# Second attention of a small transformer on one core: the scores of four heads from one 512-column product with keys widened by zeros

## The chip, the cores and the metric

One core of a Trainium2 chip runs the whole program. The metric is the device time of that core in microseconds (us); the median of several executions is used.

## The reference, cut to what matters

Input x is 8 batches of 128 tokens by 128 features, and a context of the same shape goes with it. Four blocks follow each other, each added to x: a channel attention, a mixture of 16 experts with a causal attention, the second attention (this case), and a feed-forward block with 8 routed experts. The change touches only the second attention:

```python
def _L1_xattn_ref(k, q, v, Wk, bk, Wq, bq, Wc, bc):   # k = v = context, q = layernorm(x)
    H, hd = 16, 8
    kp = k @ Wk.T + bk
    qp = q @ Wq.T + bq
    kh = kp.reshape(B, T_v, H, hd).transpose(0, 2, 1, 3)
    qh = qp.reshape(B, T_q, H, hd).transpose(0, 2, 1, 3)
    vh = v.reshape(B, T_v, H, hd).transpose(0, 2, 1, 3)
    att = jnp.einsum('bhqd,bhkd->bhqk', qh, kh) / sqrt(hd)
    att = jax.nn.softmax(att, axis=-1)
    y = jnp.einsum('bhqk,bhkd->bhqd', att, vh)
    return y.transpose(0, 2, 1, 3).reshape(B, T_q, C) @ Wc.T + bc
```

Here B is 8 and T is 128, so each batch has 16 heads of 8 features, with a 128 x 128 table of scores for each.

## The kernel before, in words

**Layout.** Each head of 8 features takes 32 rows (partitions) of the tiles ks and qs: high part, low part and marks, so that a float32 product comes out of fp32r operands. Four heads j = 0 to 3 fill the 128 partitions, and g = 0 to 3 counts the four groups, so that ks and qs are 128 partitions x 8 batches x 4 groups x 128 tokens. quarter(j) is the slice of 32 partitions of head j in its group.

**What one batch b goes through in the second attention.**

- turn_q (L1534) turns the queries, and take_qs (ACT, L690) writes them to qs.
- scores3(h), h = 2b + p with p = 0 or 1, is called once for each half of a batch (L1549). It computes the scores with queries on the partitions; they serve only to find the largest score of each row. A half is the two heads j = 2p and 2p + 1 of all four groups: eight products, each 32 rows of contraction and 128 columns. The two heads of a half go to two PSUM banks.
- softmax3(h) (DVE, L1144) reduces the two banks to the negated maxima negm. split_m (L1155, L1156) puts them as high and low part into msp.
- mark_queries (L1559, L1562) adds the maxima as extra rows to the queries, and take_marked (ACT, L705) writes qs again.
- turned_scores(h) (L1576) computes the scores again, now with keys on the partitions, in the same eight row-tiled products; exp3 (ACT, L700) takes the exponential into exT.
- attend3 (L1589, column tiles of 32), turn_y (L1596), divide (DVE), turn_divided (L1602), bring_x and project_c (L1611, L1615) end the batch.

**What sets the order.** Every engine's order is written out by hand: a counter s runs over all slots, and a function is called on its engine when s equals at_mix(b, u), at_score(b, u) or at_att(b, u). TensorE (PE) takes scores3(2b) at at_score(b, 0) and scores3(2b + 1) at at_score(b, 8). From batch 3 on, the first half's scores stand directly ahead of turned_scores of an earlier batch's second half, both behind attend3. The engine waits on semaphores in this order.

**Work of the expert block that shares time.** load_rwb (L416) and load_rwm (L424) on the SP queue bring router weights that are broadcast over the partitions from HBM: 1 MB and 0.5 MB for each batch. scale_hidden (DVE, L1099) multiplies by the first, mix(b) (DVE, L1131) by the second; project (L1476) and project_o (L1514) are the products on PE. load_rwm(7) waits for mix(6). The SP queue runs its steps strictly in turn, so a step that waits holds all steps behind it. GpSimd (POOL) is mostly busy with split_weights (L533). Its memsets (L512 to L517) stand ahead of its own loop.

Of the kernel before, what the change touches and what calls it, by code (L numbers as in the profile page):

```python
# [62 lines left out]
def build(nc, x_d, ctx_d, ctxT_d, cols_d, rows_d, kv_d, wattn_d, wqkv_d, wo_d, wa_d, wb_d, wdn_d, wg_d, out_d):  # L63
    starts, ends = {}, {}
    with ExitStack() as ctx:
# [12 lines left out]
        def sem(name):  # L78
            return ctx.enter_context(nc.semaphore(name))
# [100 lines left out]
        ry = sb("ry", [T, H1])  # L180
        yq = sb("yq", [T, H1, D1])
        yT = sb("yT", [C, 2, T])
        vT = exT[:, 0, :, :].rearrange("p a n -> p (a n)").rearrange("p (v n) -> p v n", v=2)
        bd = exT[:, 1, :, :].rearrange("p a n -> p (a n)").rearrange("p (f v i n) -> p f v i n", f=2, v=2, i=HALF)

# [63 lines left out]
        s2_ps = sem("s2_ps"); s2_ready = sem("s2_ready"); p2_ready = sem("p2_ready"); pn_ready = sem("pn_ready")  # L249
        pT2_ps = sem("pT2_ps"); pT2_ready = sem("pT2_ready"); aT_ps = sem("aT_ps"); aT_ready = sem("aT_ready")  # L250
        mix_ready = sem("mix_ready"); o_ready = sem("o_ready")
        kp_ready = sem("kp_ready"); ksT_ps = sem("ksT_ps"); ks_ready = sem("ks_ready")
        xn3_ready = sem("xn3_ready"); xn3T_ps = sem("xn3T_ps"); xn3T_ready = sem("xn3T_ready")
        qp_ready = sem("qp_ready"); qsp_ready = sem("qsp_ready"); qsT_ps = sem("qsT_ps"); qs_ready = sem("qs_ready")
# [44 lines left out]
        def routed_chunk(r):  # L299

            return (r - 1) // NROUTED * NCH + NSHARED + (r - 1) % NROUTED

        def rwm_of(b):

# [30 lines left out]
        def quarter(j):  # L335

            return slice(32 * j, 32 * j + 32)

        def score_bank(j):

            return 4 + 3 * (j % 2)
# [42 lines left out]
        @block.sync  # L384
        def _(sp):
            sp.dma_start(xr[:, bs(0), :], x_d[:, bs(0), :]).then_inc(ld_x[0], 16)
            sp.dma_start(cx[:, bs(0), :], ctx_d[:, bs(0), :]).then_inc(ld_ctx[0], 16)
            sp.dma_start(xr[:, bs(1), :], x_d[:, bs(1), :]).then_inc(ld_x[1], 16)
            sp.dma_start(cx[:, bs(1), :], ctx_d[:, bs(1), :]).then_inc(ld_ctx[1], 16)
            sp.dma_start(rowv[:, :], rows_d.partition_broadcast(128)).then_inc(ld_vec, 16)  # L390
            sp.dma_start(cxT[:, :], ctxT_d).then_inc(ld_ctxT, 16)
            sp.dma_start(wattn[:, :, :], wattn_d).then_inc(ld_attn, 16)
            sp.dma_start(wqkv[:, :, :], wqkv_d).then_inc(ld_qkv, 16)
            sp.dma_start(wo[:, :, :], wo_d).then_inc(ld_o, 16)
            sp.dma_start(wa[:, :], wa_d).then_inc(ld_up, 16)
            sp.dma_start(wb[:, :], wb_d).then_inc(ld_up, 16)
            sp.dma_start(wg[:, :], wg_d).then_inc(ld_up, 16)
            full = RUP // 128
            sp.dma_start(wdn[:, 0:full, :], wdn_d[0:full * 128, :].rearrange("(k p) c -> p k c", p=128)).then_inc(ld_dn, 16)
            sp.dma_start(wdn[0:RUP - full * 128, full, :], wdn_d[full * 128:RUP, :]).then_inc(ld_dn, 16)  # L400

            def store_rw(hf):

                rows_of = slice(HALF * E0 * hf, HALF * E0 * hf + HALF * E0)
                sp.wait_ge(rwT_ready, hf + 1)
                sp.dma_start(rw_d[rows_of, :], rwT[:, hf, :]).then_inc(rw_stored, 16)
                sp.wait_ge(rw_stored, 16 * (hf + 1))

            def load_rwb(b):

                if b < HALF:
                    sp.wait_ge(att_ready, 2)
                else:
                    sp.wait_ge(hm_ready, 4 * (b - 1))
                for q in range(4):
                    sp.dma_start(rwb[b % 2][:, 4 * q:4 * q + 4, :].rearrange("p e t -> p (e t)"),  # L416
                                 rw_d[E0 * b + 4 * q:E0 * b + 4 * q + 4, :].rearrange("e t -> (e t)").partition_broadcast(128)).then_inc(ld_rwb[b % 2][q], 16)

            def load_rwm(b):

                if b >= 2:
                    sp.wait_ge(mix_ready, b if b == NB - 1 else b - 1)
                for j in range(2):
                    sp.dma_start(rwm[rwm_of(b)][HD * j:HD * j + HD, :, :],  # L424
                                 rw_d[E0 * b:E0 * b + E0, :].rearrange("(r j) t -> j r t", j=2)[j, :, :].partition_broadcast(HD)).then_inc(ld_rwm[rwm_of(b)], 16)

            store_rw(0)
            load_rwb(2)
            load_rwb(3)
            load_rwm(0)  # L430
            load_rwm(1)
            store_rw(1)
            for b in range(HALF, NB):
                load_rwb(b)
                load_rwm(b - 2)
            load_rwm(NB - 2)
            load_rwm(NB - 1)

            def store_ww(hf):

                sp.wait_ge(wwT_ready, hf + 1)
                sp.dma_start(ww_d[E1 * hf:E1 * hf + E1, :].rearrange("e (b t) -> (e b) t", t=T), wwT[:, hf, :]).then_inc(ww_stored, 16)
                sp.wait_ge(ww_stored, 16 * (hf + 1))

            def load_ww(r):

                if r > BY_PE + 3:
                    sp.wait_ge(hid_ready, routed_chunk(r - 3) + 1)
                else:
                    sp.wait_ge(qkv_done, 4 * NB)  # L450
                for e, p, n in experts_of(r):
                    sp.dma_start(ww[p:p + n, r % 3, :], ww_d[E1 * ((r - 1) // NROUTED) + e, :].partition_broadcast(n)).then_inc(ld_ww[r % 3], 16)

            def store_out(hf):

                sp.wait_ge(out_ready, hf + 1)
                sp.dma_start(out_d[:, 512 * hf:512 * hf + 512], outT[:, hf, :]).then_inc(stored, 16)

            store_ww(0)
            for r in range(BY_PE + 1, NROUTED + 1):  # L460
                load_ww(r)
            store_ww(1)
            for r in range(NROUTED + 1, NROUTED + 4):
                load_ww(r)
            store_out(0)
            for r in range(NROUTED + 4, 2 * NROUTED + 1):
                load_ww(r)
            store_out(1)
            sp.wait_ge(stored, 32)
# [3 lines left out]
        def _(pool):  # L473
# [42 lines left out]
            link(nc.gpsimd.memset(vm[:, :, :, :], 0.0))  # L516
            link(nc.gpsimd.memset(vm[:, :, :, D1:D1 + 1], 1.0))  # L517

            def fill_vm(b):

                if b >= 2:
                    pool.wait_ge(pv_done, b - 1)
                nc.gpsimd.tensor_copy(vm[:, b % 2, :, 0:D1], cx[:, b, :].rearrange("p (h i) -> p h i", i=D1)).then_inc(vm_ready, 1)
# [29 lines left out]
                low_part(hlo[0:n, k % 3, :], hid[0:n, k % 3, :], hhi[0:n, k % 3, :]).then_inc(hlo_ready, 1)  # L553

            for s in range(LAST):
                for b in range(NB):
                    if s == at_mix(b, 82):
                        rstd_of(b + 1, 2, b, b + 1, ve_mix, rstd_mix)
                    if s == at_mix(b, 102):
                        add_bc(b)  # L560
                    if s == at_att(b, 4):
                        fill_vm(b)
                    if s == at_att(b, 44):
                        rstd_of(b + 1, 3, b, b + 1, ve_att, rstd_att)
                if s % SLOT == 0 and 0 <= s // SLOT - W4 < NCH:
                    split_weights(s // SLOT - W4)
                for hf in range(2):
                    if s == at_tail(hf, 72, 120):
                        split_x4(hf)
                for k in range(2):  # L570
                    if s == at_first(k, 8):
                        split_hidden(k)
                if s % SLOT == 0 and 2 <= s // SLOT - F4 - 1 < ON_POOL:
                    split_hidden(s // SLOT - F4 - 1)
# [275 lines left out]
        def _(dve):  # L850
# [288 lines left out]
            def softmax3(h):  # L1139
                b, p = h // 2, h % 2  # L1140
                dve.wait_ge(s3_ready, h + 1)
                if b >= 2:
                    dve.wait_ge(msp_ready, b - 1)
                V.tensor_reduce(negm[:, b % 2, 2 * p:2 * p + 2, :], score_pair.rearrange("p j (g k) -> p j g k", g=4),  # L1144
                                AX.X, ALU.max, negate=True).then_inc(mx3_ready, 1)

            def split_m(b):
# [3 lines left out]
                else:  # L1151
                    dve.wait_ge(qm_ps, b)
                dve.wait_ge(mx3_ready, 2 * b + 2)
                hi, lo = [msp[:, :, :, 3 * D1 + i].rearrange("p g j -> p j g") for i in range(2)]
                link(V.tensor_copy(hi, negm[:, b % 2, :, :]))  # L1155
                V.tensor_tensor(lo, negm[:, b % 2, :, :], hi.bitcast(F32), ALU.subtract).then_inc(msp_ready, 1)  # L1156

# [152 lines left out]
        def _(pe):  # L1310
# [226 lines left out]
            def scores3(h):  # L1537
# [6 lines left out]
                else:  # L1544
                    pe.wait_ge(mx3_ready, h)
                pe.wait_ge(qs_ready, b + 1)
                for g in range(4):
                    for j in (2 * p, 2 * p + 1):
                        last = mm(PB[score_bank(j)][:, T * g:T * g + T], qs[quarter(j), b, g, :], ks[quarter(j), b, g, :], start=True, stop=True)  # L1549
                last.then_inc(s3_ready, 1)  # L1550

            def mark_queries(b):
# [286 lines left out]
```

## Time and profile before

| | us |
|---|---|
| median of 3 runs | 237.09 (236.08 to 237.65) |
| the profiled execution | 236.62 |
| its span, first to last instruction | 234.8 |
| TensorE (PE) busy | 211.8 (90%) |
| VectorE (DVE) busy | 166.5 (71%) |
| ScalarE (ACT) busy | 112.5 (48%) |
| GpSimd (POOL) busy | 95.3 (41%) |

The mean granted TensorE clock is 0.96 of full speed. To read it: busy time says which engine has most to do, and the chain of work that ended last says what set the end. A piece of the chain is counted from the end of the piece ahead of it to its own end; so the length of a PE piece includes what the engine lost between the two. DMA issues are shown by the queue that issues them (SPq) with the time that the issue took, and elsewhere with the time from issue to landing.

### The profile page before, as it was taken

The page shows a single profiled execution, that of the slowest core. Times are in us where ns is not written, and L with a number is a line of the kernel's source. Part 1 is how long each engine was busy: PE and PEld are TensorE (multiplying, and loading weights), DVE is VectorE, ACT ScalarE, POOL GpSimd, SP SyncE. Part 2 cuts the span into 40 slices and gives each one's busy share as a digit, 9 for nine tenths or more (in the row PEclk, how much of TensorE's full clock was granted, in tenths as well). Part 3 has the DMA queues.
Part 4 walks back from the last instruction along what each step waited for, and adds up shares of the span by engine and source line. Part 5 has one row for each costly group of instructions (what it writes and reads, how often), then busy time and mean ns, then how long its engine had stood idle before and what let it go on. Part 6 is the DMA issues. An engine that isn't in the chain of part 4 may idle for free.

```text
span 234.8 us, 4985 instructions
## 1 busy us (share of the span) xinstructions
PE 211.8 (90%) x1767; PEld 180.2 (77%) x1767; DVE 166.5 (71%) x495; ACT 112.5 (48%) x259; POOL 95.3 (41%) x127
## 2 busy tenths in 40 slices
PE   1398669999999999999799999998699999999994
PEld 0356549999999998988579888887577887888872
DVE  3598797669977989858792687865765688265753
ACT  0435432423264462422263777678453745555552
POOL 7143100150096999810411021122336655655660
PEclk9999957999999999999976999999999999999998
DMA  6997000398199953300300000000024430163401
GB/s 188 349 419 228 3 6 0 96 289 155 60 260 245 242 190 89 81 12 0 89 4 0 3 3 0 3 4 0 3 48 89 122 101 6 42 189 133 152 27 45
DMA packets 19256, 23.33 MB, mean 99 GB/s; under 512 B 1792, under 2 KB 12192, under 8 KB 19104
## 3 DMA queue, kind: packets, MB, share of 16 engines
q1 hardware_dynamic: 18896, 22.94, 34.3%
q8 instruction: 14, 0.23, 0.4%
q10 hardware_dynamic: 336, 0.08, 0.2%
q14 instruction: 10, 0.08, 0.1%
HBM read 22.39 MB, written 0.62 MB: 98 GB/s over the span
## 4 chain that ended last, share of the span: by engine, by line
PE 83%; DVE 7%; ACT 3%; DMA 2%; issue 2%; ACTq 1%; POOL 0%; DVEq 0%
PE psum L1476 19%; PE psum L1657 17%; PE psum L1713 8%; PE psum L1514 7%; PE psum L1576 3%; PE psum L1589 3%; PE psum L1549 3%; DMA kv<-kv_dram 2%; PE psum L1386 2%; PE psum L1342 2%; PE psum L1491 1%; PE psum L1534 1%; PE psum L1562 1%; PE psum L1596 1%; PE psum L1504 1%
## 5 line engine op out<-in xcount | busy, mean ns | idle before, releaser
L488 POOL TENSOR_TENSOR rstd<-ve,m 128x1 f32<-128x1 f32 (+1 forms) x20 | 14.2, 712 | 96.9 <-DVE ve L872 96.8
L1476 PE MATMUL psum<-wqkv,hm 128*128 128x192 f32 x256 | 47.8, 335 | 0.0
L533 POOL TENSOR_TENSOR qs<-hm,qs 128x512 fp32r<-128x512 f32 (+1 forms) x26 | 33.9, 1302 | 22.3 <-ACT qs L746 22.1
L1476 PEld LDWEIGHTS psum<-wqkv,hm 128*128 128x128 f32 x256 | 42.3, 195 | 0.1
L1144 DVE TENSOR_REDUCE negm<-psum 128x8 f32<-128x1024 f32 x16 | 19.6, 1222 | 7.7 <-PE psum L1549 7.6
L1713 PE MATMUL psum<-qs,wdhi 128*128 128x512 f32 (+1 forms) x56 | 21.8, 401 | 0.1
L1212 DVE TENSOR_TENSOR hm<-hm,psum 128x512 f32<-128x512 f32 x19 | 13.0, 686 | 11.3 <-POOL qs L533 5.0
L700 ACT ACTIVATE exT<-psum 128x1024 f32<-128x1024 f32 x16 | 16.4, 1024 | 7.5 <-PE psum L1576 7.0
L1099 DVE TENSOR_TENSOR hm<-xn2T,exT 128x512 f32<-128x512 f32 x24 | 19.6, 817 | 0.1
L746 ACT ACTIVATE qs<-hm 128x512 fp32r<-128x512 f32 (+1 forms) x28 | 17.5, 627 | 3.3 <-DVE hm L1215 2.0
L765 ACT ACTIVATE psum<-psum 128x512 f32<-128x512 f32 x19 | 11.1, 583 | 16.5 <-PE psum L1657 16.3
L1514 PE MATMUL psum<-wo,mixT 128*128 128x128 f32 x128 | 17.4, 295 | 0.1
L1514 PEld LDWEIGHTS psum<-wo,mixT 128*128 128x128 f32 x128 | 16.6, 209 | 0.3 <-issue 0.2
L1215 DVE TENSOR_TENSOR hm<-hm,psum 128x512 f32<-128x512 f32 x19 | 13.1, 688 | 2.0
L1713 PEld LDWEIGHTS psum<-qs,wdhi 128*128 128x128 f32 (+1 forms) x56 | 10.5, 188 | 3.4 <-DVE qs L1231 0.9
L1131 DVE TENSOR_TENSOR mixT<-aT,rwm 128x1024 f32<-128x1024 f32 x8 | 10.5, 1317 | 2.8 <-issue 1.5
L1657 PE MATMUL psum<-x4hi,wahi 128*128 128x512 f32 (+1 forms) x28 | 12.0, 427 | 0.0
L1576 PE MATMUL psum<-qs,ks 32*128 32x128 f32 x128 | 10.8, 287 | 1.1 <-ACT qs L705 0.9
L1713 PE MATMUL psum<-qs,wdlo 128*128 128x512 f32 (+1 forms) x28 | 11.1, 397 | 0.0
L1657 PE MATMUL psum<-x4lo,wahi 128*128 128x512 f32 (+1 forms) x28 | 11.1, 396 | 0.0
L1657 PE MATMUL psum<-x4lo,wbhi 128*128 128x512 f32 (+1 forms) x28 | 11.1, 395 | 0.0
L1657 PE MATMUL psum<-x4hi,wblo 128*128 128x512 f32 (+1 forms) x28 | 11.0, 393 | 0.0
(235 smaller groups left out, 487.8 us busy)
## 6 DMA issues: line engine op xcount, KB each, us to landing
exT<-rw_rows SPq DMA_DIRECT2D x24, 256.0 KB, 4.8
rwm<-rw_rows SPq DMA_DIRECT2D x16, 256.0 KB, 5.8
hm<-ww_rows SPq DMA_DIRECT2D x7, 256.0 KB, 3.3
wqkv<-wqkv_dram SPq DMA_DIRECT2D x1, 1536.0 KB, 10.5
hm<-ww_rows SPq DMA_DIRECT2D x4, 224.0 KB, 3.3
wa<-wa_dram SPq DMA_DIRECT2D x1, 880.0 KB, 12.9
wb<-wb_dram SPq DMA_DIRECT2D x1, 880.0 KB, 13.3
wdn<-wdn_dram SPq DMA_DIRECT2D x1, 832.0 KB, 15.0
```

Source lines behind the costliest of these rows:

```text
L488: nc.gpsimd.tensor_tensor(dst, src, m16[:, 0:src.shape[1]], ALU.pow).then_inc(signal, 1)
L533: return nc.gpsimd.tensor_tensor(dst, src, hi.bitcast(F32), ALU.subtract)
L700: nc.scalar.activation(exT[:, b % 2, 2 * p:2 * p + 2, :], turned_pair, ACT.Exp).then_inc(ex_ready, 1)
L746: nc.scalar.activation(hhi[0:n, k % 3, :], hid[0:n, k % 3, :], ACT.Copy).then_inc(hhi_ready, 1)
L1099: V.tensor_tensor(hm[:, b % 2, 4 * q:4 * q + 4, :], bc(xn2T[:, b, :], 1, 4), weights, ALU.mult).then_inc(hm_ready, 1)
L1144: V.tensor_reduce(negm[:, b % 2, 2 * p:2 * p + 2, :], score_pair.rearrange("p j (g k) -> p j g k", g=4), AX.X, ALU.max, negate=True).then_ ...
L1215: V.tensor_tensor(hid[:, k % 3, :], hid[:, k % 3, :], PB[gate_bank(k)][:, :], ALU.mult).then_inc(hid_ready, 1)
L1476: last = mm(bank[:, 0:3 * HD], hm[:, b % 2, e, :], wqkv[:, e, :], start=(e == 0), stop=(e == E0 - 1))
L1514: last = mm(PB[5][:, 0:C], mixT[:, r, :], wo[:, r, :], start=(r == 0), stop=(r == E0 // 2 - 1))
L1576: last = mm(PB[turned_score_bank(j)][:, T * g:T * g + T], ks[quarter(j), b, g, :], qs[quarter(j), b, g, :], start=True, stop=True)
L1657: last = mm(bank[0:n, :], w[:, c0:c0 + n], x[:, cols4], start=(j == 0), stop=(j == 2))
L1713: last = mm(bank[:, :], w[0:n, ch, :], h[0:n, k % 3, :], start=(ch == 0 and j == 0), stop=(ch == NCH - 1 and j == 2))
```

## The change

scores3 no longer multiplies head by head. For each batch there is a widened copy of the keys, in which head j of group g stands on its own 32 partitions in columns 128j to 128j + 127, and everything else is zero. One product of all 128 rows of qs for group g with the 512 columns of the widened keys gives the four heads of that group. A half is now two groups (g = 2p, 2p + 1), that is two products of 128 x 128 x 512 in place of eight of 32 x 128 x 128. The PSUM banks are the same two, with group and head exchanged; softmax3 and split_m follow that order. turned_scores is unchanged.

The widened keys have two buffers, one for even and one for odd batches: kd0, new, and kd1, in two halves over cxT and sel, which are no longer used by then. GpSimd zeroes them once: kd0 with its other memsets, kd1 at slots 56 and 60. The SP queue copies the keys from ks into the diagonal blocks (widen_keys): four DMAs of 64 KB for an even batch, eight of 32 KB for an odd one. Batches 0 and 1 are copied between the load_rwb and load_rwm of batches 4 and 5, the others behind load_rwm(7); from batch 2 on a copy waits until the scores of the batch before last are done (s3_ready).

```diff
--- before.py
+++ after.py
@@ -180,6 +180,8 @@
         ry = sb("ry", [T, H1])
         yq = sb("yq", [T, H1, D1])
         yT = sb("yT", [C, 2, T])
+        kd0 = sb("kd0", [128, 4, 4, T], F32R)
+        kd1 = [over("kd1a", [128, 2, 4, T], F32R, "cxT"), over("kd1b", [128, 2, 4, T], F32R, "sel")]
         vT = exT[:, 0, :, :].rearrange("p a n -> p (a n)").rearrange("p (v n) -> p v n", v=2)
         bd = exT[:, 1, :, :].rearrange("p a n -> p (a n)").rearrange("p (f v i n) -> p f v i n", f=2, v=2, i=HALF)
 
@@ -249,6 +251,7 @@
         s2_ps = sem("s2_ps"); s2_ready = sem("s2_ready"); p2_ready = sem("p2_ready"); pn_ready = sem("pn_ready")
         pT2_ps = sem("pT2_ps"); pT2_ready = sem("pT2_ready"); aT_ps = sem("aT_ps"); aT_ready = sem("aT_ready")
         mix_ready = sem("mix_ready"); o_ready = sem("o_ready")
+        kd_zero = sem("kd_zero"); ld_kd = [sem(f"ld_kd{i}") for i in range(2)]
         kp_ready = sem("kp_ready"); ksT_ps = sem("ksT_ps"); ks_ready = sem("ks_ready")
         xn3_ready = sem("xn3_ready"); xn3T_ps = sem("xn3T_ps"); xn3T_ready = sem("xn3T_ready")
         qp_ready = sem("qp_ready"); qsp_ready = sem("qsp_ready"); qsT_ps = sem("qsT_ps"); qs_ready = sem("qs_ready")
@@ -300,6 +303,10 @@
 
             return (r - 1) // NROUTED * NCH + NSHARED + (r - 1) % NROUTED
 
+        def wide_keys(b, g):
+
+            return kd1[g // 2][:, g % 2, :, :] if b % 2 else kd0[:, g, :, :]
+
         def rwm_of(b):
 
             return 0 if b in (1, 3, 5) else 1
@@ -424,6 +431,21 @@
                     sp.dma_start(rwm[rwm_of(b)][HD * j:HD * j + HD, :, :],
                                  rw_d[E0 * b:E0 * b + E0, :].rearrange("(r j) t -> j r t", j=2)[j, :, :].partition_broadcast(HD)).then_inc(ld_rwm[rwm_of(b)], 16)
 
+            def widen_keys(b):
+
+                if b >= 2:
+                    sp.wait_ge(s3_ready, 2 * b - 2)
+                else:
+                    sp.wait_ge(kd_zero, 2 * b + 1)
+                    sp.wait_ge(ks_ready, b + 1)
+                for j in range(4):
+                    src = ks[quarter(j), b, :, :].bitcast(F32)
+                    if b % 2:
+                        for i in range(2):
+                            sp.dma_start(kd1[i][quarter(j), :, j, :].bitcast(F32), src[:, 2 * i:2 * i + 2, :]).then_inc(ld_kd[1], 16)
+                    else:
+                        sp.dma_start(kd0[quarter(j), :, j, :].bitcast(F32), src).then_inc(ld_kd[0], 16)
+
             store_rw(0)
             load_rwb(2)
             load_rwb(3)
@@ -433,8 +455,13 @@
             for b in range(HALF, NB):
                 load_rwb(b)
                 load_rwm(b - 2)
+                if b < HALF + 2:
+                    widen_keys(b - HALF)
             load_rwm(NB - 2)
             load_rwm(NB - 1)
+            sp.wait_ge(ks_ready, NB)
+            for b in range(2, NB):
+                widen_keys(b)
 
             def store_ww(hf):
 
@@ -516,6 +543,17 @@
             link(nc.gpsimd.memset(vm[:, :, :, :], 0.0))
             link(nc.gpsimd.memset(vm[:, :, :, D1:D1 + 1], 1.0))
 
+            nc.gpsimd.memset(kd0[:, :, :, :].bitcast(F32), 0.0).then_inc(kd_zero, 1)
+
+            def zero_keys(i):
+
+                if i == 0:
+                    pool.wait_ge(kp_ready, 2)
+                    pool.wait_ge(vT_ready, 2)
+                else:
+                    pool.wait_ge(rb_ready, 8)
+                nc.gpsimd.memset(kd1[i][:, :, :, :].bitcast(F32), 0.0).then_inc(kd_zero, 1)
+
             def fill_vm(b):
 
                 if b >= 2:
@@ -553,6 +591,10 @@
                 low_part(hlo[0:n, k % 3, :], hid[0:n, k % 3, :], hhi[0:n, k % 3, :]).then_inc(hlo_ready, 1)
 
             for s in range(LAST):
+                if s == at_once(56):
+                    zero_keys(0)
+                if s == at_once(60):
+                    zero_keys(1)
                 for b in range(NB):
                     if s == at_mix(b, 82):
                         rstd_of(b + 1, 2, b, b + 1, ve_mix, rstd_mix)
@@ -1141,7 +1183,7 @@
                 dve.wait_ge(s3_ready, h + 1)
                 if b >= 2:
                     dve.wait_ge(msp_ready, b - 1)
-                V.tensor_reduce(negm[:, b % 2, 2 * p:2 * p + 2, :], score_pair.rearrange("p j (g k) -> p j g k", g=4),
+                V.tensor_reduce(negm[:, b % 2, 2 * p:2 * p + 2, :], score_pair.rearrange("p g (j k) -> p g j k", j=4),
                                 AX.X, ALU.max, negate=True).then_inc(mx3_ready, 1)
 
             def split_m(b):
@@ -1151,7 +1193,7 @@
                 else:
                     dve.wait_ge(qm_ps, b)
                 dve.wait_ge(mx3_ready, 2 * b + 2)
-                hi, lo = [msp[:, :, :, 3 * D1 + i].rearrange("p g j -> p j g") for i in range(2)]
+                hi, lo = [msp[:, :, :, 3 * D1 + i] for i in range(2)]
                 link(V.tensor_copy(hi, negm[:, b % 2, :, :]))
                 V.tensor_tensor(lo, negm[:, b % 2, :, :], hi.bitcast(F32), ALU.subtract).then_inc(msp_ready, 1)
 
@@ -1544,9 +1586,9 @@
                 else:
                     pe.wait_ge(mx3_ready, h)
                 pe.wait_ge(qs_ready, b + 1)
-                for g in range(4):
-                    for j in (2 * p, 2 * p + 1):
-                        last = mm(PB[score_bank(j)][:, T * g:T * g + T], qs[quarter(j), b, g, :], ks[quarter(j), b, g, :], start=True, stop=True)
+                pe.wait_ge(ld_kd[b % 2], (128 if b % 2 else 64) * (b // 2 + 1))
+                for g in (2 * p, 2 * p + 1):
+                    last = mm(PB[score_bank(g)][:, :], qs[:, b, g, :], wide_keys(b, g).rearrange("p j t -> p (j t)"), start=True, stop=True)
                 last.then_inc(s3_ready, 1)
 
             def mark_queries(b):
```

## Rows read from the trace of the kernel before

**Rows 1.** The page: its first line, and the chain that ended last, by engine.

```profile
span 234.8 us, 4985 instructions
...
PE 83%; DVE 7%; ACT 3%; DMA 2%; issue 2%; ACTq 1%; POOL 0%; DVEq 0%
```

**Rows 2.** Groups by shape, PE: busy us, mean ns of one | idle before.

```profile
L1549 PE MATMUL psum<-ks,qs 32*128 32x128 f32 x128 | 10.6, 283 | 0.0
```

**Rows 3.** Chain, 88 to 166 us: start, length, what; scores between other full-array products.

```profile
90.56 0.59 PE psum L1549 x8
91.16 0.26 PE psum L1500
...
103.47 0.11 PE psum L1500
...
151.89 0.23 PE psum L1559
...
152.52 0.59 PE psum L1549 x8
153.11 0.27 PE psum L1602
153.38 0.59 PE psum L1576 x8
```

**Rows 4.** The same chain: scores and turned scores together, and L1529 in two places.

```profile
99.42 0.22 PE psum L1529 x2
...
128.78 0.36 PE psum L1549 x4
...
129.36 0.18 PE psum L1576 x4
...
139.04 0.43 PE psum L1529 x2
...
150.05 0.37 PE psum L1549 x4
...
150.64 0.18 PE psum L1576 x4
```

**Rows 5.** Timeline of the SP queue, 65 to 69 us: start, length, what.

```profile
65.42 2.05 SPq L416 DMA_DIRECT2D exT<-rw_rows  x4
68.38 1.26 SPq L424 DMA_DIRECT2D rwm<-rw_rows  x2
```

**Rows 6.** Timeline of DVE, the first use of batch 5's router weights.

```profile
74.28 0.96 DVE L1099 TENSOR_TENSOR hm<-xn2T,exT 128x512 f32<-128x512 f32 x1
```

**Rows 7.** Timeline: the last load of router weights, and batch 2's first scores.

```profile
113.06 1.25 SPq L424 DMA_DIRECT2D rwm<-rw_rows  x2
...
117.37 0.66 PE L1549 MATMUL psum<-ks,qs 32*128 32x128 f32 x8
```

**Rows 8.** DMA, 111 to 120 us in 40 slices; its issues: KB each, us to landing.

```profile
GB/s 0 0 0 0 0 0 0 0 0 0 0 0 0 0 0 107 262 330 339 278 216 250 223 182 93 46 5 0 0 0 0 0 0 73 0 0 0 0 0 0
...
rwm<-rw_rows SPq DMA_DIRECT2D x2, 256.0 KB, 3.8
```

**Rows 9.** Source line L452, DMAs of 32 to 256 KB: issue ns min/median/max, then landing.

```profile
L452 SPq DMA_DIRECT2D hm<-ww_rows x31: 302/413/597, 173.5 to 221.5; - x31
...
DMA to landing us min/median/max: 1.9/3.1/4.8
```

**Rows 10.** Timeline of PE: second half of batch 3's scores, first half of batch 5's.

```profile
131.13 0.66 PE L1549 MATMUL psum<-ks,qs 32*128 32x128 f32 x8
...
139.39 0.33 PE L1549 MATMUL psum<-ks,qs 32*128 32x128 f32 x2
```

**Rows 11.** Timeline of POOL: a memset of 1024 columns, and its next work but one.

```profile
50.19 0.95 POOL L516 MEMSET vm<- 128x1024 f32 x1
...
64.16 0.85 POOL L488 TENSOR_TENSOR rstd<-ve,m 128x1 f32<-128x1 f32 x1 [12.80 <-DVE ve L872]
```

**Rows 12.** Windows, 123 to 127 us: busy by engine, granted clock, DMA share, GB/s.

```profile
123.00:127.00 4.00, 4.00 (x20) 3.77 (x21) 0.73 (x4) 0.60 (x1) 0.00 (x0) 0.50 0.00 0
```

## The prediction

> **What bounds the kernel now.** I read the page first: of a span of 234.8 us, PE makes up 83% of the chain that ended last [rows 1]. So a microsecond taken from PE's own sequence is a microsecond of the kernel, unless another engine stands in at that place. Then the groups by shape: the 128 score products of L1549 are 10.6 us of PE busy time [rows 2], but these overlap, so their price has to be read from the chain. The chain between 88 and 166 us shows L1549 in two settings. Nine times it is a piece of its own, 0.59 us for eight products, between or next to other work; the first and the last stand in [rows 3]. Four times it lies mixed with the eight products of turned_scores, because a half of scores and a half of turned scores stand next to each other in PE's order; the first and the last stand in [rows 4]. In the three that are left of 16 (two alone, one mixed) another engine sets the time. Last I read the SP queue and the DMA slices, since the change puts 48 new DMAs there [rows 5, 7, 8, 9].
>
> **The new products.** The trace has no 128-row product with widened keys, but it has the same form: L1559 takes fp32r queries as weights and 512 columns of fp32r, and its piece of the chain is 0.23 us [rows 3]. Two of them are 0.46 to 0.47 us in place of 0.59. That is 0.12 us less for a half. DVE's reduction has the same size and only another order, so I cost it at nothing; its input is complete about as early as before.
>
> **What a change of tiling costs.** Behind row tiles the next full-array product pays. L1500 behind the scores takes 0.26 us, and 0.11 behind a full product; L1602 takes 0.27 us behind the scores [rows 3], for a product of the same 128 columns. That is 0.15 us. The same holds behind the column tiles of L1589: L1529 takes 0.43 us there and 0.22 elsewhere [rows 4], 0.2 us more.
>
> **Where the scores stand alone on the path.** These are batches 0 and 1 (four halves), and the second halves of batches 4, 6 and 7. Each gives 0.12 us for itself and 0.15 for the product behind it, 0.27 us. Seven of them give 1.9 us. The other two of the nine lie at batch 2: its first half is followed by row-tiled L1576 after a wait, its second half directly by L1576, so the switch stays and I take nothing for them. The second halves of batches 3 and 5 are hidden behind ACT and DVE.
>
> **Where the scores stand with the turned scores.** Now 16 products need from 128.78 to 129.54 us, and again from 150.05 to 150.82: 0.77 us for both halves [rows 4]. In all such places the scores use heads 0 and 1 and the turned scores heads 2 and 3, so four row groups are in use together. The new scores fill the array, and nothing can share it: 0.47 us for the scores, then 0.59 us for turned scores alone, as at 153.38 [rows 3], is 1.06 us. In addition scores3 stands behind attend3 here, so a full-array product comes behind column tiles, for up to 0.2 us [rows 4]. Loss: 0.29 to 0.49 us; I take 0.45, since both places where the trace shows such a switch pay nearly the whole. Four on the path lose 1.8 us. The fifth (batch 5) lies behind DVE work and is hidden; were it not, another 0.45 us. The bound below is nothing: the matmul queue might still overlap the two.
>
> The Trainium skill, page TensorE: Matmul & The Clock Gate, Part 3, says that products with 32 rows of contraction run side by side in different row groups, four of them 3.07 times as fast as in turn, and so speaks against this change. By that rule eight products in two row groups, 128 columns each, would be worth about half of their row's time, some 0.3 us, and the change would lose 0.17 us at every half: with the switch the seven halves that stand alone would come to +0.1 us in place of -1.9. The rows don't bear that out for the halves that stand alone, since 0.59 us for eight is more than the 0.47 of two full products [rows 3]; they bear it out in part for the mixed places.
>
> **The first late copy of keys.** widen_keys(2) stands on SP behind load_rwm(7), which waits for mix(6) and ends its issues at 113.06 + 1.25 = 114.31 us [rows 7]. Four DMAs of 0.41 us (the median issue of L452 [rows 9]) occupy SP until 115.95, the last one starting at 115.54. Their data stand behind the 0.52 MB of load_rwm(7), which flow until slice 27 of 0.225 us, that is 117.0 us, in some 2.5 us, about 210 GB/s [rows 8]. 256 KB at this rate take 1.25 us: 118.3 us, and 0.3 to 0.5 us more until the semaphore. Batch 2's scores start at 117.37 us [rows 7] and would now start at about 118.7: **a stall of 1.3 us**. Behind it on PE are the turned scores of batch 0, the turn of batch 7's queries and project_o(7), all of which others wait for, and PE has no idle time behind it that would absorb it. Bounds: with the fastest landing of L452, 1.9 us [rows 9], the last lands at 117.4, no stall; with the slowest, 4.8 us, at 120.3, 3.0 us of stall. Gains upstream move mix(6), the load and the scores alike.
>
> **The later copies.** An odd batch takes eight issues. Batch 5's wait for the second half of batch 3's scores, done at 131.13 + 0.66 = 131.8 us; the last of eight issues starts at 134.7 and lands by 136.6 to 139.5, needed at 139.39 [rows 9, 10]. Batch 7 has the same distance, even batches half of the issues. So I cost them at nothing; even the slowest landing costs 0.1 us each. What hides them is 8.3 us of PE work between the two scores.
>
> **The early copies.** widen_keys(0) goes between load_rwm(2) and load_rwb(5), which was issued at 65.42 us [rows 5]: four issues, 1.6 us, and 256 KB, 1.2 us of traffic. widen_keys(1), 8 x 0.41 = 3.3 us, goes behind load_rwm(3) (68.38 [rows 5]). Batch 5's weights are used from 74.28 us on [rows 6], 8.9 us after their issue and now 7.3; the slowest landing there could make DVE some 0.5 us late, but PE's use is one scaling of 0.96 us and one project later, so nothing reaches the path. Bound above: 0.5 us.
>
> **Zeroing.** 1024 columns are 0.95 us, so kd0 and the two halves of kd1 are 1.9 + 2 x 0.95 = 3.8 us of POOL. POOL is idle for 12.8 us ahead of 64.16 [rows 11]. Nothing; without this cover, up to 3.8 us.
>
> **The sum.** -1.9 (alone) + 1.8 (mixed) + 1.3 (stall) = +1.2 us. The profiled execution took 236.62 us, 1.8 more than its span, and the median of the runs shown is 0.5 above it. So 236.6 + 1.2 = 237.8, and against the median 238.3; I say 238.0.
>
> **The rivals.**
>
> *Slower: the copy for batch 2 lands late.* For it: SP can't issue it before mix(6), and the keys had long been ready; against it: nothing else is in the DMA rings at that time. At the slowest landing the stall is 3.0 us, and the sum is -1.9 + 1.8 + 3.0 = +2.9: 239.9. It decides (over 1%) from a stall of 2.5 us. The low clock works on the same side: from 123 to 127 us the granted clock was 0.50, the 1.2 GHz level, behind a stretch in which PE waited several times [rows 12]. A longer wait there can lengthen it, and each us more at half clock costs half a us.
>
> *Faster: little is lost.* The copy is in time and the queue overlaps scores and turned scores, or the switch costs nothing: -1.9 + 0 to 1.2 = -1.9 to -0.7, that is 235.0 to 236.2. For it: the 0.2 us of the switch are inferred from neighbours. Against it: 0.59 us of turned scores alone are a row.
>
> *Faster: the clock.* The new products use 128 rows where the old used 32. If this keeps the clock up around 123 us, 4 to 7 us of PE work at half clock run at full: 2 to 3.4 us less, 234.4 to 236. Against it: at that place there are only two halves of scores, and the stall brings more idle time just ahead.
>
> *No change: the copies are hidden and gains and losses cancel*, -1.9 + 1.8 = -0.1: 237.0. It lies in the forecast's own range.
>
> **How the numbers follow.** Forecast (with the hidden copies) 0.50, own range 236.6 to 239.4; late copy or longer low clock 0.25; little lost 0.15; clock better 0.10. A difference of about 1% is what a measurement of this kernel can tell from none. Over 1% slower (above 239.5) is the late copy and a little of the forecast, 0.27; over 1% faster (below 234.7) is most of the clock case and some of the little-lost case, 0.11; within 1%, 0.62. The range that leaves out 0.2: 235.0 to 240.5.
>
> **What would show it.** In the changed kernel: L1549's pieces of 0.47 us for two; L1500, L1602 and L1525 behind them at 0.11 us; the batch 3 to 7 first halves with turned scores at 1.06 to 1.25 us in place of 0.77; PE idle ahead of batch 2's first scores, ended by a DMA into kd0, of 1 to 1.5 us; no idle time ahead of batches 3 to 7 ended by a DMA; no DVE wait for exT near 74 us. I am wrong if the DMAs of widen_keys take twice the time of L452's, if full-array fp32r products at widened keys take other than 0.23 us, or if the low clock after 120 us changes its length.

## The result, and the profile after

The changed kernel takes 241.29 us (median of 4 executions) against 236.62 us (median of 4 of the kernel before): a ratio of 1.018, 95% interval 1.013 to 1.024. Medians here are over all executions of a kernel; ratios leave out those more than 1.5% above the fastest of the same kernel. The profiled execution of the changed kernel has a span of 238.8 us, 4.0 us more than before.

The page of the changed kernel, first line and chain by engine and by line; it answers [rows 1]:

```profile
span 238.8 us, 4847 instructions
...
PE 82%; DVE 6%; ACT 4%; DMA 3%; issue 2%; SPq 1%; ACTq 1%; DVEq 0%
PE psum L1518 18%; PE psum L1699 16%; PE psum L1755 8%; PE psum L1556 6%; PE psum L1618 4%; PE psum L1591 3%; PE psum L1631 3%; DMA kv<-kv_dram 2%; PE psum L1428 2%; PE psum L1576 2%; PE psum L1384 2%; PE psum L1638 1%; PE psum L1653 1%; PE psum L1533 1%; DMA kd<-ks 1%
```

A DMA and the SP queue have entered the chain. The chain of the changed kernel between 84 and 170 us shows where (start, length, what). L1556 is project_o, L1591 the wide scores, L1618 the turned scores, L1631 attend3:

```profile
86.73 1.79 PE psum L1556 x16
...
90.04 0.47 PE psum L1591 x2
90.51 0.11 PE psum L1542
...
91.92 0.64 PE psum L1591 x2
...
110.56 1.24 DVE mixT L1173
111.81 0.57 SPq L431
112.42 0.64 SPq L431
113.19 0.63 SPq L447
...
115.15 2.90 DMA kd<-ks
118.05 0.14 issue
118.19 0.71 PE psum L1591 x2
...
125.61 3.52 PE psum L1556 x16
...
130.04 1.01 PE psum L1631 x32
131.06 0.66 PE psum L1591 x2
131.72 0.59 PE psum L1618 x8
...
151.23 0.61 ACT qs L747
151.84 0.14 issue
151.97 0.66 PE psum L1618 x8
```

Three things are to be seen. From 110.56 to 118.19 us the path leaves PE: mix(6), load_rwm(7), four issues of batch 2's copy, its landing. Behind it project_o(7) takes 3.52 us at half clock, as it did before, but from S to C (marks below) the time grows from 9.7 to 11.1 us, since the low clock now lasts longer. And a mixed place takes 0.66 + 0.59 = 1.25 us; it answers the 0.77 us of [rows 4].

To compare runs I cut each trace at four marks that every kernel has, read from its chain: A is the start of project_o(3) (87.25 us before, 86.73 after), S the end of the first half of batch 2's scores (118.03 and 118.89), C the start of the first attend3 (127.76 and 130.04), L the start of the last attend3 (165.58 and 169.63). The time ahead of A is not compared: the granted clock falls there too, in every profile, from 25 to 31 us on for 7 to 14 us, and A lies between 86.2 and 88.9 us whatever the kernel.

| kernel | A to S | S to C | C to L | L to end |
|---|---|---|---|---|
| before | 30.8 | 9.7 | 37.8 | 69.2 |
| after | 32.2 | 11.1 | 39.6 | 69.2 |
| e1, copy early | 30.0 | 7.0 | 39.6 | 70.2 |
| e2, old products | 33.0 | 11.0 | 37.8 | 69.2 |
| e3, wide at 0 and 1 | 30.1 | 9.7 | 37.8 | 69.3 |
| e4, old products, copy early | 30.8 | 9.7 | 37.8 | 69.2 |
| e5, wide at 0 to 2, copy early | 30.0 | 7.0 | 37.8 | 69.2 |
| e6, wide at 2 alone, copy early | 30.7 | 7.0 | 40.8 | 69.2 |
| e7, e1 with a third product | 30.0 | 7.0 | 39.7 | 69.2 |
| e8, e1 with scores moved | 30.0 | 7.0 | 45.0 | 70.4 |
| e9, e5 with 32 rows at 2 | 30.1 | 9.6 | 37.8 | 69.4 |
| e10, e5 with the copy late | 32.0 | 9.6 | 40.8 | 69.3 |

The stretches agree to 0.1 us wherever the same thing happens in them, so each column can be read as an effect of its own. The loss of the change is +1.4, +1.4 and +1.8 us; with the 0.5 us by which A lies earlier, that is the 4.0 us of the spans. Another 0.6 us lies outside the span: the profiled execution took 2.4 us more than its span, and 1.8 before. What this is stays open.

### The profile page after: what moved, and what is told of

Read it like the earlier page. It is cut to its first block, busy times and chain, and to the rows that moved or that the text cites. A ratio compares the mean times of both kernels' runs of the same rounds, so it can differ in the third digit from the quotient of the medians.

```text
span 238.8 us, 4847 instructions
## 1 busy us (share of the span) xinstructions
PE 214.1 (90%) x1671; PEld 179.4 (75%) x1671; DVE 167.7 (70%) x495; ACT 112.0 (47%) x259; POOL 98.9 (41%) x130
## 4 chain that ended last, share of the span: by engine, by line
PE 82%; DVE 6%; ACT 4%; DMA 3%; issue 2%; SPq 1%; ACTq 1%; DVEq 0%
PE psum L1518 18%; PE psum L1699 16%; PE psum L1755 8%; PE psum L1556 6%; PE psum L1618 4%; PE psum L1591 3%; PE psum L1631 3%; DMA kv<-kv_dram 2%; PE psum L1428 2%; PE psum L1576 2%; PE psum L1384 2%; PE psum L1638 1%; PE psum L1653 1%; PE psum L1533 1%; DMA kd<-ks 1%
## 5 line engine op out<-in xcount | busy, mean ns | idle before, releaser
L807 ACT ACTIVATE psum<-psum 128x512 f32<-128x512 f32 x19 | 11.1, 582 | 17.7 <-PE psum L1699 17.6
L1556 PE MATMUL psum<-wo,mixT 128*128 128x128 f32 x128 | 17.5, 295 | 0.1
L1556 PEld LDWEIGHTS psum<-wo,mixT 128*128 128x128 f32 x128 | 16.6, 209 | 0.3 <-issue 0.2
L1618 PEld LDWEIGHTS psum<-qs,ks 32*128 32x128 f32 x128 | 9.2, 200 | 6.4 <-issue 5.2
L1755 PEld LDWEIGHTS psum<-qs,wdhi 128*128 128x128 f32 (+1 forms) x56 | 10.5, 188 | 3.4 <-DVE qs L1273 0.9
L1618 PE MATMUL psum<-qs,ks 32*128 32x128 f32 x128 | 11.3, 297 | 1.6 <-ACT qs L747 1.1
L1755 PE MATMUL psum<-qs,wdlo 128*128 128x512 f32 (+1 forms) x28 | 11.1, 397 | 0.0
L1699 PE MATMUL psum<-x4lo,wahi 128*128 128x512 f32 (+1 forms) x28 | 11.1, 396 | 0.0
```

The source lines that it names most:

```text
L1556: last = mm(PB[5][:, 0:C], mixT[:, r, :], wo[:, r, :], start=(r == 0), stop=(r == E0 // 2 - 1))
L1618: last = mm(PB[turned_score_bank(j)][:, T * g:T * g + T], ks[quarter(j), b, g, :], qs[quarter(j), b, g, :], start=True, stop=True)
L1699: last = mm(bank[0:n, :], w[:, c0:c0 + n], x[:, cols4], start=(j == 0), stop=(j == 2))
L1755: last = mm(bank[:, :], w[0:n, ch, :], h[0:n, k % 3, :], start=(ch == 0 and j == 0), stop=(ch == NCH - 1 and j == 2))
```

## The experiments

**e1: the copy of batch 2 early.** One step moves on the SP queue:

```diff
             load_rwm(NB - 2)
-            load_rwm(NB - 1)
             sp.wait_ge(ks_ready, NB)
-            for b in range(2, NB):
+            widen_keys(2)
+            load_rwm(NB - 1)
+            for b in range(3, NB):
                 widen_keys(b)
```

> The changed kernel with one step moved: the copy of batch 2's keys is issued on the SP queue ahead of the last load of router weights (which waits for mix(6)) in place of behind it. Theory (a late copy, and a low clock that it lengthens): TensorE no longer waits for a DMA ahead of batch 2's first scores, which gives back 2.0 us, and the low granted clock behind it shrinks from 10.2 us to the 6.8 us of the kernel before, which gives 1.4 us more: about 237.9 us for 241.3. Rival (the clock goes by the form of the products or by chance, not by the wait): only the 2.0 us come back and the low stretch stays 10.2 us, 239.3 us.

Measured: 236.94 us, ratio to before 0.997 (0.993 to 1.001), 4.4 us less than the changed kernel. The wait for the DMA is gone, and the low clock did not shrink to that of the kernel before: it vanished. Windows of e1 and of the kernel after, from S to C (busy by engine, then granted clock, DMA share, GB/s):

```profile
118.80:125.80 7.00, 6.55 (x60) 5.54 (x64) 5.68 (x13) 3.57 (x7) 0.10 (x1) 1.00 0.28 64
```

```profile
119.50:130.00 10.50, 10.13 (x52) 8.68 (x52) 5.30 (x13) 3.58 (x6) 0.00 (x0) 0.51 0.17 39
```

From S to C the same work takes 7.0 us at full clock and 11.1 us in the kernel after, 10.5 of them at a mean of 0.51. So the late copy costs more than either expectation: 2.2 us from A to S and 4.2 us from S to C. (The two spans differ by only 3.3 us, because in the profile of e1 A lies 2.1 us later and the last DMA takes 1.0 us longer.)

**e2: the old products with all copies and waits.** scores3, softmax3 and split_m are as before the change; the waits for the copies stay.

> The changed kernel with all its copies, zeroing and waits for the copies, but with the old row-tiled products in scores3 (the widened keys are waited for and not read). Theory: the stall of 2 us ahead of batch 2 and the longer low clock (1.4 us) stay, the losses and gains of the products go: about 240 us, and 0.77 us for 16 products wherever scores and turned scores are mixed. Rival (the wide products themselves are most of the loss, the wait only a shift of idle time): about 237 us.

Measured: 240.81 us, ratio 1.019 (1.013 to 1.024). Almost the whole loss is there without a single wide product in the kernel. The waits of PE in e2, 88 to 166 us (us in total, times, longest):

```profile
PE psum L1592 <- DMA kd<-ks: 2.1, 1, 2.1
```

The low clock from S to C is the longer one again, 11.0 us. The mixed places are back at 0.77 us, and C to L at 37.8.

**e4: old products and the early copy.**

> Both edits: old row-tiled products, all copies and waits kept, and the copy of batch 2's keys ahead of the last load of router weights. Theory: what is left of the change is only zeroing and 48 DMAs, all hidden: 236.6 us as before, low clock 6.8 us. Rival (the copies cost by themselves, through DMA traffic or the SP queue, other than by the one wait): 237.5 us or more, with DVE waiting for router weights near 74 us or TensorE waiting for copies at batches 5 and 7.

Measured: 237.75 us, ratio 1.002 (0.999 to 1.005). The median alone would fit the rival's 237.5 us; the profile doesn't: every stretch is that of the kernel before to 0.1 us, VectorE doesn't wait for router weights, and TensorE doesn't wait for a copy. Zeroing and 48 DMAs cost nothing that shows in the stretches once none is late.

**e3: wide products at batches 0 and 1 alone.** All other batches compute as before the change.

> Widened keys and 512-column products for batches 0 and 1 alone, whose scores stand between full-array products; batches 2 to 7 with the old row-tiled products and no copies. Theory: four halves gain what the changed kernel's chain shows there, 0.8 us together, and nothing is lost: 0.8 us under the kernel before, 235.8 us. Rival (the gain at batches 0 and 1 is only a shift, given back at the waits around 110 us that go through DVE and GpSimd): the time of the kernel before, 236.6 us.

Measured: 235.50 us, ratio 0.996 (0.992 to 0.999). The stretch from A to S loses 0.7 us, nothing else moves. The gain is real and passes the waits on VectorE and GpSimd around 110 us.

**e5: wide products at batches 0 to 2, batch 2's copy early.**

```diff
+        WIDE = (0, 1, 2)
...
+                if b in WIDE:
...
+                    for g in (2 * p, 2 * p + 1):
...
+                else:
+                    for g in range(4):
+                        for j in (2 * p, 2 * p + 1):
...
```

> Widened keys and 512-column products for batches 0, 1 and 2 alone, batch 2's copy ahead of the last load of router weights; batches 3 to 7 with the old row-tiled products and no copies. In the runs so far the stretch from batch 2's first scores to the first attend3 takes 9.7 us with the old products at batch 2 and 7.0 us with the wide ones in time, because the low granted clock is missing there. Theory A (the wide products of batch 2, just ahead of the place where the clock falls, keep it up): 7.0 us there, 0.8 us less for batches 0 and 1, and the 37.8 us of the old products behind it: 236.8 - 0.8 - 2.7 = 233.3 us. Rival B (the clock was kept by something else in that run, as the later wide products or the place of its windows): 9.7 us there, 236.0 us.

Measured: 234.93 us, ratio 0.989 (0.984 to 0.994); only e7, with two executions, has the same ratio. All stretches are as theory A had them; A to L is 74.8 us against 78.3. The median gains 2.0 us, less than the profile's 3.5: the profiled execution is the fastest of the six, and the mean granted clock of single executions was 0.953 to 0.985, so the low clock probably does not stay away in each of them. Where it fell in the others isn't known.

**e6: wide products at batch 2 alone.**

> Widened keys for batch 2 alone, copied early; all other batches with the old products and no copies. Theory A (batch 2's wide products alone keep the granted clock up): the stretch behind batch 2's first scores takes 7.0 in place of 9.7 us, no gain at batches 0 and 1: 234.1 us. Rival B (it needs the wide products of batches 0 and 1 as well, or it is chance): the time of the kernel before, 236.8 us.

Measured: 237.26 us, ratio 1.001 (0.997 to 1.006). The profile shows theory A at its place, 7.0 us from S to C, and then a low clock at another, windows of e6:

```profile
119.00:126.00 7.00, 6.50 (x57) 5.43 (x56) 5.64 (x14) 3.69 (x8) 0.21 (x1) 1.00 0.02 4
158.00:165.00 7.00, 7.00 (x61) 6.04 (x61) 2.42 (x16) 4.06 (x6) 0.55 (x1) 0.54 0.00 0
```

That costs 3.0 us from C to L, and the gain is gone: by its median the run is where rival B had it. So a clock kept up at one place can fall at a later one, here behind a wait of 0.65 us for ScalarE. The same wait stands in e5, where the clock stays up.

**e9: 32 rows at batch 2.**

```diff
+                    r = quarter(0) if b == 2 else slice(0, 128)
-                        last = mm(..., qs[:, b, g, :], wide_keys(b, g)...)
+                        last = mm(..., qs[r, b, g, :], wide_keys(b, g)[r, :, :]...)
```

> Wide products for batches 0 to 2 with the early copy, but at batch 2 the four products of 512 columns use 32 rows only, in place of 128: this kernel leaves out three of four heads in the row maxima of batch 2's scores; number, columns and time of the products stay. It asks what of the wide products keeps the granted clock up behind 118 us. Theory A (the number of rows in use): the low stretch between 118 and 128 us is back, 9.7 us from batch 2's first scores to the first attend3 in place of 7.0, and a median of 236 to 237 us. Theory B (the columns that stream without a gap, or the timing): still no low stretch there, 7.0 us, and the 235 us of the kernel with all rows.

Measured: 237.30 us, ratio 0.995 (0.990 to 1.001). The times do not separate the theories: the interval overlaps that of e5 (0.984 to 0.994), and the six executions in the ratio have their middle at 235.4 us, near the 235 of theory B. The profile is on the side of theory A. Windows of e9 and of e5, S to C:

```profile
116.60:126.20 9.60, 9.23 (x60) 8.20 (x64) 5.91 (x15) 3.47 (x7) 0.00 (x0) 0.64 0.01 3
```

```profile
116.40:123.40 7.00, 6.53 (x61) 5.49 (x64) 5.64 (x14) 3.62 (x7) 0.15 (x1) 1.00 0.02 4
```

Up to batch 2's first scores the two kernels have the same instructions at the same distances from A (29.46 us in e9, 29.45 in e5). Behind that, more than the rows differs, against what the expectation took for granted. The chain at the second half, e9 and then e5:

```profile
118.09 0.42 PE psum L1598
118.52 0.16 PE psum L1629 x2
118.68 0.08 PE psum L1598
118.75 0.26 PE psum L1629 x6
```

```profile
118.04 0.61 PE psum L1597 x2
118.66 0.59 PE psum L1628 x7
```

The 32-row products run mixed with the turned scores, 0.92 us for both in place of 1.20, and the first half takes 0.66 us in place of 0.55. And in these 32 rows only 128 of the 512 columns of the widened keys are not zero, so the values differ too. e9 shows that the low clock comes back without the wide products' full rows; whether the rows, the values or the 0.3 us less of TensorE work does it is not separated.

**e10: e5 with the copy late.**

> Wide products for batches 0 to 2 as in the best kernel so far (median 234.9 us), with batch 2's copy behind the last load of router weights again; nothing else differs. Theory (the late copy is the main loss of the change: a stall of 2.2 us on TensorE, and a low clock behind it of 10 us that costs some 4 us more): 241 us. Rival (the stall alone, the low clock was chance in the two profiles that had it): 237.1 us.

Measured: 242.34 us, ratio 1.023 (1.014 to 1.031), against 0.989 for e5. One DMA step at another place in a queue moves the time by 3.4%, some 8 us. PE waits 1.9 us for the DMA; in the profile a low clock follows, and a second one near 163 us:

```profile
121.00:128.50 7.50, 7.13 (x39) 5.88 (x38) 4.99 (x10) 3.48 (x6) 0.00 (x0) 0.56 0.01 3
162.00:169.00 7.00, 6.81 (x60) 5.98 (x61) 2.76 (x18) 4.40 (x8) 0.84 (x2) 0.56 0.01 2
```

The rival is refuted, but the second low stretch was in no expectation, and why a low clock comes there in e6, e8 and e10 and not in e1, e5 or e7 is open.

**e7: a third product in the second halves.**

```diff
+                if b >= 3 and p == 1:
+                    last = mm(PB[score_bank(g)][:, :], qs[:, b, g, :], wide_keys(b, g)..., start=True, stop=True)
```

> The changed kernel with the early copy of batch 2, and the last product of the second half of batches 3 to 7 issued twice (0.23 us of TensorE each, 1.15 us in all). Theory (the second halves' shorter scores uncovered ScalarE's take_marked, for which turned_scores waits, so their gain was lost): the added product is hidden at batches 3, 6 and 7 and costs at batches 4 and 5 at most, and the stretch from the first attend3 to the last goes from 39.6 to 39.8 to 40.1 us. Rival (TensorE's own sequence is the path everywhere, and the wide products cost more there for another reason): 39.6 + 4 to 5 x 0.23 = 40.5 to 40.7 us.

Measured: 234.29 us with two executions, ratio 0.989 (0.984 to 0.995) where e1 has 0.997. That two executions are faster than e1 was in no expectation. Between the two profiles the 3.3 us lie ahead of A (86.3 us here, 88.8 in e1) and in the last DMA (1.0 us), not where the product was added; the cause is open. The stretch from C to L answers the question: 39.73 us against 39.59. Five products of 0.23 us cost 0.14 us. The chain of e7 at batch 6's end, and of e1 at the same place:

```profile
149.62 0.40 PE psum L1607 x4
150.01 0.51 PE psum L1592 x2
150.53 0.23 PE psum L1594
150.75 0.11 PE psum L1647
150.87 0.59 PE psum L1621 x8
```

```profile
151.91 0.41 PE psum L1605 x4
152.35 0.61 ACT qs L748
152.96 0.14 issue
153.09 0.66 PE psum L1619 x8
```

In e1 the turned scores wait for ScalarE's take_marked (0.61 + 0.14 us), and PE's own work between (two products and L1645) is shorter. In e7 PE's work just fills the gap, and the turned scores start almost equally long behind the start of that part of mark_queries: 1.25 us in e7, 1.18 in e1.

**e8: the first halves' scores between full-array products.** From batch 3 on, scores3(2b) is called at at_score(b, 3), behind bring_x, in place of at_score(b, 0).

> The changed kernel with the early copy of batch 2, and the first half of the scores of batches 3 to 7 moved in TensorE's order from between attend3 and turned_scores to behind bring_x, between full-array products. Theory (a wide product behind column tiles pays some 0.2 us for the switch): turned_scores then follows attend3, tiles behind tiles, and the stretch from the first attend3 to the last goes from 39.6 to about 38.8 us, the time from 236.9 to 236.1. Rival (the later scores make VectorE's maxima late, and the second half waits for them; or the switch isn't what costs): 39.6 us or more.

Measured: 241.61 us, ratio 1.017 (1.011 to 1.023). The rival holds, and more. The chain of e8 around 138 us:

```profile
138.05 0.42 PE psum L1654 x2
138.47 0.48 PE psum L1592 x2
...
138.97 1.23 DVE negm L1187
140.20 0.22 DVE st L1212
...
140.73 0.26 DVE ry L1205
...
141.01 0.30 DVE yq L1208
...
141.35 0.33 PE psum L1645
```

The wide scores do take 0.48 us there in place of 0.66, so the switch is what costs 0.2 us. But VectorE's reduction now comes so late that the division of the batch before stands behind it, and PE waits for that in each period. From C to the turns at L1668 (155.74 us in e8, 154.76 in e1) this costs 2.5 us, and a low clock near 161 us adds 2.9.

## Why the prediction was wrong, point by point

**The direction of the sum was right, its size not.** I forecast +1.2 us and no measurable change, 238.0 us with 240.5 as the upper end; it is 241.29. In the profile, term by term:

| term | forecast | measured | from |
|---|---|---|---|
| scores that stand alone | -1.9 | -1.0 | batches 0 and 1: -0.8; batches 4, 6 and 7: -0.2 |
| scores with turned scores | +1.8 | +1.9 | 4 x 0.48 |
| stall at batch 2 | +1.3 | +2.2 | A to S, after against e1 |
| low clock behind it | not in the sum | +1.4 | S to C, after against before |
| sum | +1.2 | +4.5 | less 0.5 by which A lies earlier: the 4.0 of the spans |

**The first late copy: right place, the term too small.** The path is the one described: mix(6), load_rwm(7), four issues, landing, PE's wait. I priced an issue at 0.41 us after L452 [rows 9]. The four issues took 0.6 us each, as nearly all 48 did (median 0.60, four of them 0.9 to 1.4); the timeline of the SP queue after the change:

```profile
113.19 2.57 SPq L447 DMA_DIRECT2D kd<-ks  x4
...
134.51 0.58 SPq L445 DMA_DIRECT2D kd1a<-ks  x1
```

The last DMA was issued at 115.15 and landed 2.90 us later. The stall is 2.2 us in place of 1.3. That is below the 2.5 us from which I had a late copy decide, and the time went over 1% all the same: the stall alone doesn't explain it. The nearer row was there: load_rwm's DMA has the same 512-byte pieces and takes 1.25 us for two [rows 7]. I took the median of DMAs with whole rows. The copies of 32 KB cost the same 0.6 us of issue as those of 64 KB, so the two halves of kd1 doubled the SP time of the odd batches; that stayed hidden.

**The clock: the step that failed.** I named a longer low clock as something that works on the side of the slow rival, and a better clock as a rival with a chance of 0.10, and priced neither into the sum. My own sign of being wrong came true: the low clock behind 120 us went from 6.8 us to 10.2. Both mechanisms are real and belong to one question: what the stall at batch 2 does to the clock behind it. With wide products at batch 2 and no stall the low stretch is absent (e1, e5, e6, e7, e8: 7.0 us from S to C), 2.7 us less than the 9.7 of the old products, as the rival with the better clock had it (2 to 3.4 us); with the stall it is there even behind wide products (e10: 9.6 us), or longer than before (after, e2: 11.0 to 11.1 us). The late copy thus costs 6.3 us in the profile, 2.2 as a wait and 4.2 as clock, and 4.4 us between the medians of the kernel after and e1. The 1.4 us that the kernel after loses against before from S to C are only the difference between two low clocks.

**Where the scores stand alone: half right.** At batches 0 and 1 four halves gave 0.7 to 0.8 us (A to S in e3 and e5), forecast 1.1. A first half gave its 0.27 us: 0.47, and 0.11 for L1542 behind it. A second half takes 0.64 us at batch 0, where TensorE waits 0.2 us for VectorE's maxima of the first half, so that the faster product can't start sooner. At batch 1 it takes 0.52 us; the 0.05 us above 0.47 are not explained. At the second halves of batches 4, 6 and 7, forecast 0.8 us, there came 0.2 us: e1's periods differ from before by +0.37, +0.46 and +0.47 us, where the mixed place alone explains 0.49. The work I made shorter was the cover of ScalarE's take_marked (e7). I had read the chain, in which ScalarE did not appear at these places, and did not ask what lay just under it.

**Where the scores stand with the turned scores: right.** Forecast 0.45 us for each of four; measured 1.25 - 0.77 = 0.48 us. 0.66 against 0.47 us for two products is the switch behind column tiles, 0.2 us as forecast. The Trainium skill, page TensorEngine Tiling (Array Packing), section Key Properties, says that a change of tiling mode drains the engine; the pieces of 0.66 us behind L1631 in the kernel after and 0.48 us behind L1654 in e8 agree. Batch 5's mixed place was hidden, as forecast.

**The rule on row tiles.** The Trainium skill, page TensorE: Matmul & The Clock Gate, Part 3, measures 3.07 times for four products of 32 rows side by side; my estimate from it was a loss at each half. e3 shows a gain of 0.7 us where the scores stand alone; the loss of 0.48 us is only where four row groups were in use together.

**The later and early copies, zeroing: right, nothing on the path** (e4). Batch 5's last copy was issued at 139.32 us and landed after 1.9, needed at 142.6: 1.4 us to spare. VectorE did not wait for exT, and the three memsets of 3.7 us ended at 54.2 us, 9.3 us ahead of POOL's next work.

**What is shown and what is argued.** Shown by single edits: the price of the late copy (after to e1, e5 to e10, e4 to e2), of the products at batches 0 and 1 (e3), of the later batches (e1 against e5 from C to L), the cover (e7). That the stall brings the low clock back (after against e1, e10 against e5) or makes it longer (e2 against e4) is shown at this one place, by three pairs of profiles. That the wide products of batch 2, in time, keep the clock up rests on five profiles with them (7.0 us from S to C) against three of kernels with the old products and no stall (9.7 us). The mean clocks of single executions, which take in the stretch ahead of A as well, agree: 0.983 to 0.985 is reached in e1, e5, e7 and e8, while no execution of the kernel before, of e3, e4 or e9 is above 0.971 (nor is one of e6). That it is the rows in use is argued from one profile of e9, in which values and overlap differ as well. Where the next low stretch falls is not explained.

## What to carry to other kernels

A DMA that is put at the end of an in-order queue inherits every wait ahead of it: look for the step ahead of it that waits longest, and put the copy whose data are long ready in front of that one. Price a stall on TensorE with what it does to the clock behind it; here, in the profiles, the clock cost twice the wait (4.2 against 2.2 us). And before a piece of PE's chain is made shorter, ask which other engine's work runs beneath it, since this is all that the gain can be.

## What the runs showed of the hardware

- The clock fell or stayed up with the form of four products of 512 columns: 9.6 us at a mean granted clock of 0.64 with 32 rows, 7.0 us at 1.00 with 128 (e9 and e5). The Trainium skill, page TensorE: Matmul & The Clock Gate, Part 1, says that the gate goes by how busy PE has been. These two profiles suggest that the rows in use count as well, but the values multiplied and the overlap with other products differed too. The levels are 1.2 and 2.4 GHz.
- Issuing a DMA within SBUF with pieces of 512 bytes took 0.6 us on the SP queue, for 32 KB as for 64 KB, against a median of 0.41 us for L452's. With nothing else in the queues it landed in 1.9 to 2.1 us (medians), behind 0.5 MB of router weights the last one landed in 2.9.
- A product of 512 fp32r columns with 128 rows takes 0.23 us, and eight products of 32 rows and 128 columns take 0.59 us alone, but 16 of them in four row groups 0.77 us.
